# A new order of the calls on all engines of a fused three-layer kernel

## The reference

```
x = x + cross_attention(layernorm(x), ctx, ctx, mask)   # 32 heads of 32, 8 kv groups, 257 context rows
x = x + s4(layernorm(x))                                # long convolution with a kernel made from
                                                        # Lambda, p, q, Vc, Ct, Bp, D, log_step
x = x + experts(layernorm(x))                           # q = x Wq; scores = q keys; top 16 of 64, softmax -> gate
                                                        # z = x A (64 experts x rank 8), z * gate, times B, * 2
```

## Time and profile before

| | |
|---|---|
| median of 3 runs | 1288.33 us |
| the profiled execution | 1290.52 us, span 1288.6 us |
| TensorE busy | 1232.9 us (96%) |
| weight loads | 1083.1 us (84%) |
| ScalarE busy | 1122.9 us (87%) |
| VectorE busy | 959.7 us (74%) |
| GpSimd busy | 825.4 us (64%) |
| granted TensorE clock, mean | 0.992 |
| DMA | 166.38 MB, 129 GB/s in the mean |

### The profile page before, as it was taken

The page is one execution under the profiler, slowest core; times in us unless marked ns, Lnnn a source line. Parts: engine busy times, 40 slices in busy tenths (PEclk is TensorE's granted clock), DMA queues, the critical chain, the costliest instruction groups (busy, mean ns, idle before and its releaser), DMA issues.

```text
span 1288.6 us, 41515 instructions
## 1 busy us (share of the span) xinstructions
PE 1232.9 (96%) x13676; PEld 1083.1 (84%) x13676; DVE 959.7 (74%) x3424; ACT 1122.9 (87%) x3337; POOL 825.4 (64%) x1259
## 2 busy tenths in 40 slices
PE   3679999999999999999999999999999999999997
PEld 2558888888888888888888888888888888888886
DVE  6977777777777777877777777677777877877753
ACT  5889999998999999999999999989999999999841
POOL 4447676776667677666767766676777666777520
PEclk9979999999999999999999999999999999999999
DMA  7443443443344444434544433453443344444210
GB/s 237 134 127 93 151 155 122 130 133 125 119 148 152 124 130 132 129 123 141 155 122 131 147 124 118 134 154 123 131 151 123 122 128 154 132 125 132 61 60 33
DMA packets 150103, 166.38 MB, mean 129 GB/s; under 512 B 58217, under 2 KB 116082, under 8 KB 149890
## 3 DMA queue, kind: packets, MB, share of 16 engines
q1 hardware_dynamic: 149890, 163.72, 40.9%
HBM read 128.50 MB, written 34.08 MB: 126 GB/s over the span
## 4 chain that ended last, share of the span: by engine, by line
PE 76%; DVE 5%; DMA 4%; POOL 4%; ACT 4%; issue 3%; SPq 2%; DVEq 0%; ACTq 0%; POOLq 0%
PE ps_p L562 22%; PE ps_p L633 15%; PE ps_p L661 12%; PE ps_p L648 12%; PE ps_p L594 8%; PE ps_s L574 7%; ACT pr L840 2%; DMA dn<-den 2%; DMA xq<-in_x 1%; POOL lastp L1093 1%; DVE ms L1387 1%; SPq L381 1%; ACT pts L772 1%; DMA vl<-in_ctx 1%; POOL lastp L1103 1%
## 5 line engine op out<-in xcount | busy, mean ns | idle before, releaser
L840 ACT ACTIVATE pr<-ms,negmax 128x256 f32<-128x256 f32 x1024 | 512.6, 504 | 17.3 <-DVE negmax L1387 17.3
L1387 DVE CUSTOM_DVE_ANT_0 ms<-ps_s,neg_mask,last 128x256 f32<-128x256 f32 x1024 | 447.0, 473 | 7.1 <-PE ps_s L574 6.2
L772 ACT ACTIVATE pts<-ps_p 128x512 f32<-128x512 f32 x512 | 298.3, 590 | 45.8 <-PE ps_p L562 29.1
L562 PE MATMUL ps_p<-ident,pr 128*128 128x128 f32 x2048 | 296.5, 280 | 10.4 <-ACT pr L840 5.1
L562 PEld LDWEIGHTS ps_p<-ident,pr 128*128 128x128 f32 x2048 | 229.1, 142 | 48.0 <-issue 17.4
L840 ACT ACTIVATION_READ_ACCUMULATOR pr<-ms,negmax 128x1 f32 x1024 | 199.6, 195 | 0.0
L1061 POOL TENSOR_TENSOR kt<-kr,kt 128x512 fp32r<-128x512 f32 x128 | 164.9, 1288 | 24.1 <-ACT kt L772 24.1
L648 PE MATMUL ps_p<-wa_hi,ut_hi 128*128 128x288 f32 x512 | 159.6, 312 | 1.4 <-DVE ut_lo L1203 1.4
L648 PE MATMUL ps_p<-wa_lo,ut_hi 128*128 128x288 f32 x512 | 151.8, 296 | 0.0
L648 PE MATMUL ps_p<-wa_hi,ut_lo 128*128 128x288 f32 x512 | 151.7, 296 | 0.0
L1203 DVE TENSOR_TENSOR ut_lo<-ps_p,ut_hi 128x512 fp32r<-128x512 f32 x128 | 87.7, 690 | 74.8 <-ACT ut_hi L772 74.5
(11 more groups left out here) (139 smaller groups left out, 2584.6 us busy)
## 6 DMA issues: line engine op xcount, KB each, us to landing
cx<-in_ctx SPq DMA_DIRECT2D x128, 256.0 KB, 3.9
kr<-in_keys SPq DMA_DIRECT2D x128, 256.0 KB, 3.0
xq<-in_x SPq DMA_DIRECT2D x32, 512.0 KB, 4.3
turn_q<-xq SPq DMA_DIRECT2D x32, 512.0 KB, 2.9
qx<-turn_q SPq DMA_DIRECT2D x128, 128.0 KB, 2.9
xr<-in_x SPq DMA_DIRECT2D x32, 512.0 KB, 3.9
out_x<-tmp SPq DMA_DIRECT2D x32, 512.0 KB, 3.2
dn<-den SPq DMA_DIRECT2D x512, 2.0 KB, 2.3
```

The lines of the kernel that those rows point to most:

```text
L562: mm = pe.transpose(into[:, j * P:(j + 1) * P], source, ident[:, :])
L772: return act.activation(out, in_, ACT.Copy, scale=scale)
L840: act.activation(pr[:, b % 2, g, :], ms[:, n % MS, :], ACT.Exp, bias=negmax[:, n % MS:n % MS + 1], scale=-1.0, accum_out=den[:, b, g:g + 1 ...
L1387: dve.tensor_tensor_reduce(ms[:, n % MS, :], ps_s[:, g % GPH, g // GPH * SW:(g // GPH + 1) * SW], neg_mask[:, 0:SW], 1.0, last[:, it % 2, ...
```

## The change

All five `iteration` functions, the heads and the tails have their calls in a new order. No call is added or removed, apart from how the calls of `experts`, `expand` and `convolve` cut their products in the tail. Some banks change. Cut to what the prediction speaks of:

```diff
 BANKS = {
-    "pair": (1, 0, 0, 1, 0, 2, 0, 3, 1, 0, 1, 1, 0, 3, 1, 0,),
-    "out": (0, 1,),
+    "pair": (1, 0, 0, 1, 0, 2, 0, 3, 2, 0, 1, 1, 0, 3, 1, 0,),
+    "out": (0, 2,),
...
-    "sums": (3,),
-    "dft": (1,),
+    "sums": (0,),
+    "dft": (0,),
     "rows": (3,),
-    "strip": (2, 3, 2,),
-    "w": (1, 3, 0, 2, 1, 0, 3, 2, 1, 1, 2, 3, 0, 2, 2, 1,),
+    "strip": (1, 0, 1,),
+    "w": (3, 2, 1, 3, 2, 1, 3, 2, 1, 3, 2, 0, 3, 2, 1, 2,),
 }
```

SP's loop, without the `if on(...)` lines, old and new:

```diff
-turn_last(it); store(it-3); move_den(it-1,2); load_context(it-1,2); load_residual(it-1); load_context(it,0)
-move_den(it-1,3); load_last(it+1); store_q(it+1); load_keys(it+1,0); move_q(it+1); load_keys(it+1,1)
-load_context(it,3); load_keys(it+1,2); load_x(it+2); load_context(it,1); move_den(it,1); store_last(it+1)
-move_den(it,0); load_keys(it+1,3)
+load_keys(it+1,0); turn_last(it); load_residual(it-1); store(it-3); move_den(it-1,2); load_context(it-1,2)
+move_den(it-1,3); load_context(it,0); load_context(it,3); load_last(it+1); store_q(it+1); load_keys(it+1,1)
+load_keys(it+1,2); move_q(it+1); move_den(it,1); load_x(it+2); load_context(it,1); load_keys(it+1,3)
+move_den(it,0); store_last(it+1)
```

TensorE's loop in the same way (P: `pair_chunk`, A: `attend`, S: `scores`, X: `experts` with half and range, O, U, Z: chunks; calls without a mark are of tile `it`, ' is `it - 1` and '' is `it - 2`):

```diff
-P11' S0 P12' P13' P14' X1''(0:8) P15' P0 A4' S1 P1 A5' A6' A7' P2 X0''(0:5) P3 O0' X0''(5:8) O1' S2 P4
-gated_chunk'' A0 A1 P5 P6 P7 expand'' P8 U0' S3 P9 U1' convolve' P10 Z0' A2 A3 Z1'
+P11' S0 P12' P13' X1''(0:3) P14' P15' X1''(3:8) P0 P1 A4' A5' S1 A6' A7' P2 X0''(0:3) P3 O0' X0''(3:8) P4 O1'
+gated_chunk'' A0 A1 S2 P5 P6 P7 expand'' U0' P8 S3 U1' P9 convolve' Z0' P10 A2 A3 Z1'
```

ScalarE's loop, the part from exponential 16 on:

```diff
-exp 16, copy 6, exp 17, k_high(it,3), copy 7, exp 18, last_exp 0, exp 19, exp 20, row_norm', exp 21, last_exp 1
-exp 22, exp 23, u_high'(0), copy 8, u_high'(1), exp 24, q_high 0, exp 25 to 27, k_high 0, exp 28, k_high 1, copy 9
-k_high 2, exp 29, q_high 1, exp 30, copy 10, last_exp 2, z_high'(0), z_high'(1), copy 11, output 1, exp 31
-last_exp 3
+copy 6, row_norm', exp 16, copy 7, exp 17, exp 18, k_high 0, u_high'(0), exp 19, copy 8, exp 20, u_high'(1)
+exp 21, k_high 1, last_exp 2, k_high 2, exp 22, exp 23, q_high 0, exp 24, copy 9, exp 25, exp 26, q_high 1
+exp 27, z_high'(0), exp 28, copy 10, last_exp 3, exp 29, z_high'(1), output 1, copy 11, exp 30, exp 31
```

VectorE's loop from maximum 11 to 16 (the new order has `gated(1)` behind `out_half(0)` and ahead of maxima 14 and 15, and `gated(0)` behind them), and the heads of SP, TensorE and VectorE up to the first tile's attention:

```diff
-maximum 11 to 13, route_step 5 to 8, maximum 14, route_step 9, maximum 15, out_half'(0), gated''(1)
-gated''(0), out_half'(1), maximum 16, u_stats'(0)
+maximum 11, maximum 12, route_step 5 to 8, maximum 13, route_step 9, out_half'(0), gated''(1), maximum 14
+maximum 15, gated''(0), out_half'(1), gated_low'', u_stats'(0), u_stats'(1), maximum 16, u_stats'(2)
...
-load_x(0); load_router(); load_mask(); load_s4(); load_wide(); load_weight(0); load_weight(1)
-load_last(0); load_context(0, 2); clear_kernel(); load_keys(0, 0); load_context(0, 0); load_weight(2)
-store_q(0); load_keys(0, 1); load_last(1); move_q(0); load_x(1); load_weight(3); load_keys(0, 2)
+load_s4(); load_x(0); load_wide(); load_router(); clear_kernel(); load_keys(0, 0); load_last(0)
+load_weight(0); load_mask(); load_weight(1); store_q(0); load_weight(2); load_keys(0, 1); move_q(0)
+load_x(1); load_keys(0, 2); load_weight(3); store_last(0); load_keys(0, 3); load_last(1)
...
-weight_chunk(1, 1); cauchy_sums(); weight_chunk(2, 0); weight_chunk(2, 1); weight_chunk(3, 0)
-scores(0, 0); pair_chunk(0, 0); pair_chunk(0, 1); weight_chunk(3, 1); scores(0, 1); pair_chunk(0, 2)
+weight_chunk(1, 1); cauchy_sums(); weight_chunk(2, 0); weight_chunk(2, 1); scores(0, 0)
+weight_chunk(3, 0); weight_chunk(3, 1); pair_chunk(0, 0); pair_chunk(0, 1); scores(0, 1); pair_chunk(0, 2)
...
-q_stats(0, 0); q_stats(0, 1); q_stats(0, 2); s4_step(); s4_step(); s4_step(); s4_step(); s4_step()
-s4_step(); s4_step(); router_low(); weight_low(0, 0); s4_step(); weight_low(0, 1); s4_step(); q_turn(0, 0)
-weight_low(1, 0); s4_step(); q_stats(1, 0); q_stats(1, 1); q_turn(0, 1); q_stats(1, 2); s4_step()
-weight_low(1, 1); s4_step(); weight_low(2, 0); maximum(0, 0); maximum(0, 1); maximum(0, 2); maximum(0, 3)
+s4_step(); s4_step(); q_stats(0, 0); q_stats(0, 1); s4_step(); q_stats(0, 2); s4_step(); s4_step()
+s4_step(); s4_step(); router_low(); s4_step(); weight_low(0, 0); q_turn(0, 0); s4_step(); weight_low(0, 1)
+q_stats(1, 0); q_turn(0, 1); q_stats(1, 1); weight_low(1, 0); s4_step(); weight_low(1, 1); q_stats(1, 2)
+s4_step(); weight_low(2, 0); maximum(0, 0); maximum(0, 1); weight_low(2, 1); maximum(0, 2); maximum(0, 3)
+maximum(0, 4); weight_low(3, 0); maximum(0, 5); maximum(0, 6); maximum(0, 7); s4_step(); maximum(0, 8)
```

More of the change, by code:

```diff
@@ L694, in iteration @@
                     experts(it - 2, 0, 1, 3)
-                    experts(it - 2, 0, 3, 5)
                 pair_chunk(it, 3)
@@ L699, in iteration @@
                 if on(it - 2):
+                    experts(it - 2, 0, 3, 5)
                     experts(it - 2, 0, 5, 6)
                     experts(it - 2, 0, 6, 8)
+                pair_chunk(it, 4)
                 if on(it - 1):
                     out_chunk(it - 1, 1)
-                scores(it, 2)
-                pair_chunk(it, 4)
                 if on(it - 2):
@@ L709, in iteration @@
                 attend(it, 1)
+                scores(it, 2)
                 pair_chunk(it, 5)
@@ L766, in _ @@
-            experts(31, 0, 0, 8); gated_chunk(31); expand(31, 0, 0, 4); expand(31, 1, 0, 4)
+            pair_chunk(30, 11); scores(31, 0); pair_chunk(30, 12); pair_chunk(30, 13); pair_chunk(30, 14)
+            experts(29, 1, 0, 1); experts(29, 1, 1, 3); experts(29, 1, 3, 4); experts(29, 1, 4, 6)
+            experts(29, 1, 6, 8); pair_chunk(30, 15); pair_chunk(31, 0); attend(30, 4); attend(30, 5); scores(31, 1)
+            attend(30, 6); attend(30, 7); pair_chunk(31, 1); experts(29, 0, 0, 1); experts(29, 0, 1, 3)
@@ new lines, in _ @@
+            pair_chunk(31, 2); experts(29, 0, 3, 5); experts(29, 0, 5, 6); pair_chunk(31, 3); out_chunk(30, 0)
+            experts(29, 0, 6, 8); out_chunk(30, 1); pair_chunk(31, 4); gated_chunk(29); attend(31, 0); attend(31, 1)
+            scores(31, 2); pair_chunk(31, 5); pair_chunk(31, 6); pair_chunk(31, 7); expand(29, 0, 0, 4)
+            expand(29, 1, 0, 2); expand(29, 1, 2, 3); expand(29, 1, 3, 4); pair_chunk(31, 8); u_chunk(30, 0)
+            scores(31, 3); pair_chunk(31, 9); u_chunk(30, 1); convolve(30, 0, 0, 4); convolve(30, 1, 0, 1)
@@ new lines, in _ @@
+            convolve(30, 1, 1, 8); z_chunk(30, 0, 0); pair_chunk(31, 10); z_chunk(30, 1, 0); attend(31, 2)
+            attend(31, 3); pair_chunk(31, 11); pair_chunk(31, 12); pair_chunk(31, 13); experts(30, 1, 0, 1)
+            experts(30, 1, 1, 3); experts(30, 1, 3, 4); pair_chunk(31, 14); pair_chunk(31, 15); attend(31, 4)
+            attend(31, 5); attend(31, 6); attend(31, 7); experts(30, 1, 4, 6); experts(30, 1, 6, 8)
+            experts(30, 0, 0, 1); experts(30, 0, 1, 3); experts(30, 0, 3, 5); out_chunk(31, 0); experts(30, 0, 5, 6)
@@ new lines, in _ @@
+            experts(30, 0, 6, 8); out_chunk(31, 1); gated_chunk(30); expand(30, 0, 0, 4); expand(30, 1, 0, 2)
+            u_chunk(31, 0); u_chunk(31, 1); expand(30, 1, 2, 3); expand(30, 1, 3, 4); convolve(31, 0, 0, 4)
+            convolve(31, 1, 0, 1); convolve(31, 1, 1, 8); z_chunk(31, 0, 1); z_chunk(31, 1, 1); experts(31, 1, 0, 1)
+            experts(31, 1, 1, 3); experts(31, 1, 3, 4); experts(31, 1, 4, 6); experts(31, 1, 6, 8)
+            experts(31, 0, 0, 1); experts(31, 0, 1, 3); experts(31, 0, 3, 5); experts(31, 0, 5, 6)
@@ L768, in _ @@
+            experts(31, 0, 6, 8); gated_chunk(31); expand(31, 0, 0, 4); expand(31, 1, 0, 2); expand(31, 1, 2, 3)
+            expand(31, 1, 3, 4)
         @block.scalar
@@ L1147, in iteration @@
             def iteration(it, odd):
+                k_low(it, 1)
                 if on(it - 1):
@@ L1542, in iteration @@
                 maximum(it, 12)
-                maximum(it, 13)
                 if on(it - 2):
@@ L1556, in iteration @@
                     gated(it - 2, 1)
+                maximum(it, 14)
+                maximum(it, 15)
+                if on(it - 2):
                     gated(it - 2, 0)
```

404 lines of the change are left out of this document (193 added, 211 removed).

## The result

The kernel after the change is slower by half a per cent: 1293.25 us in the median of 20 runs (1287.73 to 1298.26) against 1287.2 us (1280.84 to 1291.74) for the kernel before on the same chip; ratio 1.0052, interval 1.0038 to 1.0066. The forecast was 1272 us, faster, with a range of 1263 to 1283. It was wrong in sign.

The account below looks back on a forecast made before the run. It took TensorE's stream without holes to bound the loop, and ScalarE and VectorE to pace the head. Terms -10.2 + 0 - 6 - 0.3 = -16.5 us off the 1288.3 us median gave 1272 us, range 1263 to 1283 us.

Parts of the forecast that it names:

- TensorE's order: Loop: two fewer scores and attend groups and recut experts save 0.35 us a period, -10.2 us (0 to -15.4).
- stalls in the loop: Loop, under the bank change: one bank wait goes, small stalls come at the gated chunk; 0 us (-6 to +6).
- head: Before the loop: VectorE's earlier q turns bring the first exponential from 42.43 to near 36.5 us; -6 us (0 to -10).
- tail: After the loop: experts 30 spread between the last pair chunks shrink one wait at the gated chunk; -0.3 us.
- The forecast's own sign of being wrong: Loop and head: forecast wrong if the period lies above 37.3 us or the head is less than 3 us shorter.
- set old and new stalls equal: Loop: stalls were not summed row by row but taken as unchanged, 0 us.
- are transfers of 2 to 4 us that I cost at nothing: Loop: the residual's load, two denominators moves and context loads swap places within a few microseconds; no cost.
- the S4 steps: Head: six small VectorE operations moved behind maximum 7 could be slowed beside GpSimd, eating some 4 us of the 6.
- hardly grown: From first exponential to loop: the head's 6 us gain is carried along without much increase, ScalarE being busy 64.1 of 71.4 us.
- Rival 3: Loop: ScalarE held behind the u chunk makes it slower; with 1 us added a period, +12.5, 1301 us; chance 0.07.
- Rival 2: Loop and head: stalls go too, period 0.2 us under the forecast's, head gains 9 us; 1263 us; chance 0.09.

Follow-up runs that it names:

- a1: Kernel after with GpSimd's low half of key 2 moved back ahead of the row scales and last_shift; 1283.41 us, ratio 0.9966 to before.
- e2: Kernel after with only the context transfer moved first in SP's loop, key 2's low half left late; 1285.11 us, ratio 0.9976 to before.
- d1: Kernel after with key 2's low half early on GpSimd and the context transfer first in SP's loop; 1272.68 us, ratio 0.9894 to before.

## Why the prediction was wrong

Against the forecast's own terms, all in the profiled executions:

| term | forecast | measured |
|---|---|---|
| TensorE's order | -10.2 | -7.0 (37.27 to 37.03 us, 29 times) |
| stalls in the loop | 0 (-6 to +6) | +15.1 (0.22 to 0.74 us a period) |
| head | -6 | -11.2 |
| tail | -0.3 | +3.0 |
| sum | -16.5 | about 0 |

The forecast's own sign of being wrong came, a period above 37.3 us. The medians lose 6 us more than the traces. They are not resolved by term; the square of a1, e2 and d1 puts some 20 us on the two losses together, where the trace of after has 15.1.

**The step that failed** is the one that "set old and new stalls equal", and in it the sentence that the moved transfers "are transfers of 2 to 4 us that I cost at nothing". The denominators' and context transfers were never laid against the call that needs them. In the period of the earlier trace rows, before the change, SP's timeline and TensorE's have

```profile
601.83 0.58 SPq L362 DMA_DIRECT2D cx<-in_ctx  x1
```

```profile
605.61 0.64 PE L594 MATMUL ps_p<-pts,cx 128*32 128x128 f32 x16
```

The transfer landed after 3.0 us, which left 0.8 us. In the median of the 29 periods the lead was 4.6 us and the landing came after 3.0; after the change they are 3.9 and 3.7 us. Two transfers more in front of it used up the room; which of the two did it, no run tells, nor why the landing itself takes longer. d1 and e2 show that an early issue takes the loss away. The same sum passed over GpSimd's loop as "the low parts of the keys earlier", which is true for keys 1, 3 and 0 and false for key 2: that one went from ahead of `last_shift(it, 0)` to behind it. The bounds of +6 us were too narrow because they came from no mechanism.

**The port of VectorE and GpSimd was seen and applied in one place only.** Operations on 8 columns that took 4.59 us beside GpSimd stand in the earlier trace rows. The forecast used them against the S4 steps in the head and did not ask where else a GpSimd operation would come to lie beside a small VectorE one. For the S4 steps the worry was too large: the step moved behind maximum 7 took 2.67 us beside GpSimd's reading at 43.74, and the head gained 11.2 us all the same.

```profile
44.02 2.67 DVE L1248 TENSOR_TENSOR x<-x 128x8 f32<-128x8 f32 x6
```

```profile
43.74 1.27 POOL L1067 TENSOR_TENSOR kt<-kr,kt 128x512 fp32r<-128x512 f32 x1
```

The same rule of the Trainium skill, "SBUF — State Buffer", section SBUF: two separate sides, says who can meet: a VectorE operation with two SBUF inputs against a GpSimd operation that reads SBUF, and whoever starts first keeps the port for the whole instruction. The trace agrees on both points: the two TENSOR_TENSOR operations on `dn` reach 1291 ns, about the 1.29 us of GpSimd's own, and the RECIPROCAL between them, with one input, stays at 352 to 353 ns in all 28. Four of the 28 lay wholly inside GpSimd's operation, and the operation behind each was held until that ended. One of them:

```profile
525.06 0.35 DVE L1450 RECIPROCAL dn<-dn 128x32 f32<-128x32 f32 x1
525.45 0.90 DVE L1452 TENSOR_TENSOR dn<-dn 128x32 f32<-128x32 f32 x1
```

```profile
525.01 1.29 POOL L1067 TENSOR_TENSOR kt<-kr,kt 128x512 fp32r<-128x512 f32 x1
```

The order of the starts decides: the second TENSOR_TENSOR took 1.29 us when it started at 639.53, 0.04 us behind `k_low(it, 2)`, and 0.19 us when it started at 941.89, 0.02 us ahead of it.

**TensorE's order** was right in mechanism and gave two thirds of what was forecast. Block by block over the undisturbed periods, the transposes became 0.32 us shorter per period (10.70 to 10.38), against 0.37 forecast. And experts of half 1 cut in 9 and 15 cost 1.29 + 2.08 = 3.37 us (709.88 less 708.59, 712.75 less 710.67) where 24 in a row cost 3.29 in the median: +0.08 for the +0.02 taken. The forecast had priced the cut by half 0, which is cut in both kernels and costs 3.33 us before and 3.32 after. Scores, attend, expand and the convolution are the same within 0.01 us. That leaves 0.24 of 0.35 us a period.

**Head.** The places were right and each came earlier than worked out: VectorE and ScalarE of after, against the earlier trace rows:

```profile
24.41 0.70 DVE L1399 STREAM_TRANSPOSE qr<-qx 128x512 f32<-128x512 f32 x1
25.03 2.39 DVE L1248 TENSOR_TENSOR x<-x,un 128x512 f32<-128x512 f32 x2
...
28.66 0.71 DVE L1399 STREAM_TRANSPOSE qr<-qx 128x512 f32<-128x512 f32 x1
```

```profile
35.23 0.50 ACT L846 ACTIVATE pr<-ms,negmax 128x256 f32<-128x256 f32 x1
```

Turn 0 came at 24.41, 2.4 us under the 26.8 of its predecessor's end, where I had allowed 1.4; the first exponential at 35.23 for 36.5. From there the gain grew from 7.2 to 11.2 us where "hardly grown" was forecast: between 42.43 and 113.85 us TensorE is busy for 59.67 us and not 56.08. The other kernels with this head and loop have 7.2 to 9.8 us, so 6 us was low but this trace flatters it.

**Tail.** Sized by the one wait that would shrink; the row scale that GpSimd was given two calls later was not followed to its user.

**The rivals.** Rival 3 had the right sign and the wrong place. ScalarE is indeed held, but in the experts of half 0, and not behind the u chunk. Rival 2's length of the undisturbed period, about 37.0 us, is what d1 reached: 37.09 us, and 1272.68 us for the whole kernel. The 1272 us of the forecast is what this change gives once two calls are put earlier. The agreement with d1 is partly luck. In d1's trace the order gave -7.0 us for -10.2, the stalls of before went too (-4.6 for 0), the head gave -8.7 for -6 and the tail +3.9 for -0.3: four misses that cancel.

## What to carry to other kernels

When calls are reordered, lay out for every moved call what it is released by and who stands behind it on each engine: a GpSimd operation moved behind the wait that also releases a small two-input VectorE operation can meet it, as it did here in 18 of 29 periods. Do the same for each transfer: its lead at the consumer less its landing time was 0.8 us in the period shown and 1.3 us in the median here, and two transfers put in front of it used that up in two thirds of the periods. A change can win in the sum of its blocks and still lose: here two calls put elsewhere turned a loss of 0.5% into a gain of 1.1%.

## What was not expected of the hardware

A VectorE operation of 0.19 us took up to 1.29 us beside one GpSimd operation, and one such stretch in a period cost about 1.0 us of that period (38.16 against 37.14 us in the mean) on an engine that is busy for 78% of the loop. Cutting a run of 24 matrix products in two, with transposes between, cost 0.08 us in half 1 of the experts, where half 0, cut the same way, is only 0.03 us above the uncut run. What is still open is why after's median lies 3 us above its trace and before's 3 us below its own: by the theory more of after's periods meet in the other executions, which no trace here shows.
